# W y of the batch statistics from halves of W and y in three fp32r products, beside one fp32 product, in an attention block on one core

## The reference

```python
x = x + _L0_conv_ref(_gn(x), ...)
# within _L0_conv_ref, per image (n = 4096 positions, c = 256, ci = 128 channels):
g_x  = g_w x + g_b                      # 128 x 4096
attn = softmax(x^T x, axis=-1)          # 4096 x 4096
y    = attn g_x                         # 128 x 4096, transposed back
wy   = W_w y + W_b                      # 256 x 4096
mean, var = wy.mean((0, 2, 3)), wy.var((0, 2, 3))    # over all four images
return (wy - mean) * rsqrt(var + 1e-5) * gamma + beta + x
```

## Time and profile before

| | us |
|---|---|
| median of three runs | 2064.85 (2064.07 to 2065.0) |
| the profiled execution's own time | 2062.11 |
| its span | 2060.4 |
| TensorE busy | 2016.9 (98%) |
| VectorE, ScalarE, GpSimd busy | 1542.7, 1112.0, 788.6 |
| W y for the statistics (L1467), busy as recorded | 50.0 + 14.3, in 98 + 28 recorded instructions |

### The profile page before, as it was taken

One profiled execution on the slowest core, in us unless ns is written; L12 is line 12 of the kernel. 1 busy time (PEld: TensorE's weight loads), 2 busy tenths in 40 slices (PEclk: granted clock), 3 DMA queues, 4 the chain that ended last, 5 costly groups with the idle time before them and its releaser, 6 DMA issues.

```text
span 2060.4 us, 28131 instructions
## 1 busy us (share of the span) xinstructions
PE 2016.9 (98%) x9348; PEld 1453.2 (71%) x9348; DVE 1542.7 (75%) x3116; ACT 1112.0 (54%) x2311; POOL 788.6 (38%) x608
## 2 busy tenths in 40 slices
PE   5999999999999999999999999999999999999999
PEld 4787777666688777766678777766668877776444
DVE  6777777877777777786777777787777777777777
ACT  4345555566444545547554555556644455655657
POOL 3012233469601123358821123246970202345750
PEclk9999999999999999999999999999999999999999
DMA  3222233555511333464622223455561132346998
GB/s 143 106 86 96 102 113 128 179 179 194 169 67 69 126 103 105 160 205 152 219 83 90 83 102 122 128 184 164 188 191 67 67 123 91 103 128 188 344 346 326
DMA packets 107503, 299.90 MB, mean 146 GB/s; under 512 B 11488, under 2 KB 11872, under 8 KB 93536
## 3 DMA queue, kind: packets, MB, share of 16 engines
q1 hardware_dynamic: 107360, 298.11, 42.6%
HBM read 157.55 MB, written 140.51 MB: 145 GB/s over the span
## 4 chain that ended last, share of the span: by engine, by line
PE 89%; ACT 3%; DVE 3%; POOL 2%; issue 2%; DMA 1%; SPq 0%; DVEq 0%; ACTq 0%
PE bank L1397 18%; PE bank L1320 12%; PE bank L1322 12%; PE bank L1321 12%; PE bank L1373 9%; PE bank L1401 5%; PE bank L1403 5%; PE bank L1402 5%; PE bank L1556 3%; PE bank L1467 3%; PE bank L1327 1%; PE bank L1355 1%; PE bank L1356 1%; DVE plo L1127 1%; ACT phi L933 1%
## 5 line engine op out<-in xcount | busy, mean ns | idle before, releaser
L933 ACT CAST phi<-bank 128x512 fp32r<-128x512 f32 x480 | 281.4, 586 | 678.7 <-PE bank L1373 678.3
L1096 DVE TENSOR_SCALAR_CACHE_REDUCE ring<-bank 128x512 f32<-128x512 f32 x560 | 386.2, 690 | 257.0 <-PE bank L1322 200.0
L1320 PE MATMUL bank<-xh 128*128 128x512 f32 (+3 forms) x1152 | 513.4, 446 | 4.0 <-POOL xl L783 3.6
L1322 PE MATMUL bank<-xh,xl 128*128 128x512 f32 (+3 forms) x1152 | 435.4, 378 | 0.0
L1321 PE MATMUL bank<-xl,xh 128*128 128x512 f32 (+3 forms) x1152 | 432.7, 376 | 0.0
L1127 DVE TENSOR_TENSOR plo<-bank,phi 128x512 fp32r<-128x512 f32 x480 | 329.5, 687 | 136.6 <-ACT phi L933 109.4
L892 ACT ACTIVATE ring<-ring,nmax 128x512 f32<-128x512 f32 x464 | 334.7, 723 | 1.0
L812 POOL TENSOR_TENSOR fy_c<-fy_c,maxrow 128x512 f32<-128x512 f32 x192 | 247.6, 1291 | 197.2 <-DMA fy_c<-spill 197.2
L812 POOL TENSOR_TENSOR fy_d<-fy_d,maxrow 128x512 f32<-128x512 f32 x181 | 234.4, 1297 | 230.0 <-DMA fy_d<-spill 230.0
L1373 PEld LDWEIGHTS bank<-ident,ring 128*128 128x128 f32 x1856 | 224.1, 140 | 133.1 <-issue 80.0
L1373 PE MATMUL bank<-ident,ring 128*128 128x128 f32 x1856 | 279.4, 273 | 7.9 <-DVE plo L1127 7.2
(11 more groups left out here) (155 smaller groups left out, 2760.6 us busy)
## 6 DMA issues: line engine op xcount, KB each, us to landing
spill<-ring SPq DMA_DIRECT2D x108, 1024.0 KB, 4.4
fy_c<-spill SPq DMA_DIRECT2D x200, 256.0 KB, 4.0
fy_d<-spill SPq DMA_DIRECT2D x188, 256.0 KB, 4.2
ring<-x_dram SPq DMA_DIRECT2D x42, 512.0 KB, 5.5
lbuf<-spill SPq DMA_DIRECT2D x60, 256.0 KB, 3.8
yd<-yn SPq DMA_DIRECT2D x24, 256.0 KB, 3.3
out_dram<-ring SPq DMA_DIRECT2D x10, 512.0 KB, 3.3
fx_a<-x_dram SPq DMA_DIRECT2D x8, 512.0 KB, 6.9
```

Source lines behind the costliest of these rows:

```text
L933: nc.scalar.copy(phi[:, HI_BUF[n], :], whole(p)).then_inc(hi_made, 1)
L1096: last = nc.vector.tensor_scalar(slot_tile(u, t), src, 1.0, None, ALU.mult, ALU.max, accum_out=rowm[:, t, c:c + 1])
L1320: nc.tensor.matmul(dst, xh[:, k, rows], xh[:, k, cols], start=(k == 0), stop=False)
L1322: last = nc.tensor.matmul(dst, xl[:, k, rows], xh[:, k, cols], start=False, stop=(k == K - 1))
```

## The change

W y for the statistics is made as Wh yh + Wl yh + Wh yl, three fp32r products for each half, instead of one fp32 product. Wh and Wl are made once in the head (ScalarE a copy, GpSimd a subtraction, into wws). For each y, ScalarE casts y to yh (`make_yh`, into yn_r, which is the room of yn; for block 7 into maxrow_r, the room of maxrow) at the head of step 4, and GpSimd takes yl = y - yh (`make_yl`, into lsb_r, the room of lsb) at a place in its queue given by YL_AT. For the y of blocks 0 to 6 VectorE now writes y into row j of colmax in every image (so far in the last one only), and this row is stored. The last y of the last image keeps its fp32 product, as does the final pass, for which W is loaded once more in the last image (WW_BACK). The first half of wy moves from step 5 to step 6, and its bn_stats from step 7 to step 8.

```diff
--- before.py
+++ after.py
@@ -261,7 +261,7 @@
 assert max(NEXT_PRODUCTS) + 1 < TILES + FIRST_EXP
-INVERT_AT, TAKE_AT, SCALE_AT, WY_AT = 0, 1, 2, (5, 9)
+INVERT_AT, TAKE_AT, SCALE_AT, WY_AT = 0, 1, 2, (6, 9)
 LATE = [1] * NB
@@ -324,6 +324,12 @@
              for j in range(1, NB)}
+YL_AT = {j: min(w for w, p in enumerate(LEFT) if p > (j + 1) * TPB + SCALE_AT + LATE[j] + 7) for j in range(NB - 1)}
+WW_BACK = 5 * TPB
+assert WW_BACK > max(G_AT) + 2
+YL_OF = {w: j for j, w in YL_AT.items()}
@@ -457,11 +463,20 @@
             plo = scoped("plo", [P, LOS, W])
+            yn_r = scoped("yn_r", [P, W])
+            maxrow_r = scoped("maxrow_r", [P, W])
+            lsb_r = scoped("lsb_r", [P, W])
+            wgs = scoped("wgs", [P, K, 2 * CI])
         fx_a = sb("fx_a", [P, K, N])
         keep = sb("keep", [P, HIS + LOS, W])
+        yn = sb("yn", [P, W])
+        maxrow = sb("maxrow", [P, W])
+        lsb = sb("lsb", [P, W])
+        wwb = sb("wwb", [P, 2, C])
+        wwt = wwb[:, 0, :]
         ring = sb("ring", [P, SLOTS - 1, T, W])
@@ -490,18 +505,15 @@
         lbuf = sb("lbuf", [P, LBUFS, W])
-        lsb = sb("lsb", [P, W])
-        maxrow = sb("maxrow", [P, W])
-        yn = sb("yn", [P, W])
         ident = sb("ident", [P, P])
         gavg = sb("gavg", [P, P])
-        wgs = sb("wgs", [P, K, 2 * CI], F32R)
         wgh, wgl = wgs[:, :, 0:CI], wgs[:, :, CI:2 * CI]
-        wwt = sb("wwt", [P, C])
+        wws = sb("wws", [P, 2, C], F32R)
+        ww_raw = lsb[:, 0:C]
         bgc = sb("bgc", [P, 2])
         vecs = sb("vecs", [P, 3, K])
-        bst = sb("bst", [P, K, NB, 6])
+        bst = colmax[:, 0, 0:K * NB * 6].rearrange("p (k c s) -> p k c s", k=K, c=NB)
         mv = sb("mv", [P, K, 2])
@@ -580,6 +593,10 @@
         y_stored = sem("y_stored")
+        ww_hi = sem("ww_hi")
+        ww_lo = sem("ww_lo")
+        yh_made = sem("yh_made")
+        yl_made = sem("yl_made")
         wy_made = sem("wy_made")
@@ -646,7 +663,11 @@
-            return colmax[:, j, :] if b == B - 1 and j < NB - 1 else yn[:, :]
+            return colmax[:, j, :] if j < NB - 1 else yn[:, :]
+        def yh_home(j):
+            return (yn_r if j < NB - 1 else maxrow_r)[:, :]
@@ -686,7 +707,7 @@
                 sp.wait_ge(y_made, b * NB + j + 1)
-                sp.dma_start(yd[bass.ds(b, 1), :, j * W:(j + 1) * W].rearrange("b p w -> p (b w)"), yn[:, :]
+                sp.dma_start(yd[bass.ds(b, 1), :, j * W:(j + 1) * W].rearrange("b p w -> p (b w)"), y_home(b, j)
                              ).then_inc(y_stored, 16)
@@ -718,6 +739,9 @@
                     store_y(b - 1, NB - 1)
+                if not more and s == WW_BACK:
+                    sp.wait_ge(g_made, B * (2 * NB))
+                    sp.dma_start(wwt, ww).then_inc(ww_back, 16)
                 if not more and s in FIN_AT:
@@ -741,7 +765,7 @@
             sp.dma_start(wraw, wg.rearrange("(k p) c -> p k c", p=P)).then_inc(consts_in, 16)
-            sp.dma_start(wwt[:, :], ww).then_inc(consts_in, 16)
+            sp.dma_start(ww_raw, ww).then_inc(consts_in, 16)
             sp.dma_start(bgc[:, :], bg).then_inc(consts_in, 16)
@@ -788,10 +812,22 @@
+            def make_yl(b, j):
+                pool.wait_ge(yh_made, b * NB + j + 1)
+                if b + j > 0:
+                    pool.wait_ge(left_summed, b * (NB - 1) + j)
+                nc.gpsimd.tensor_tensor(lsb_r[:, :], y_home(b, j), yh_home(j).bitcast(F32), ALU.subtract
+                                        ).then_inc(yl_made, 1)
             def image(b, more):
+                if b > 0:
+                    make_yl(b - 1, NB - 1)
                 for c in range(len(NEXT_G), NB):
                 for w in range(NLEFT):
+                    if w in YL_OF:
+                        make_yl(b, YL_OF[w])
                     if more and w == AHEAD[GROUP_AT + 4]:
@@ -831,6 +867,8 @@
                 make_gl(0, c)
+            pool.wait_ge(ww_hi, 1)
+            nc.gpsimd.tensor_tensor(wws[:, 1, :], ww_raw, wws[:, 0, :].bitcast(F32), ALU.subtract).then_inc(ww_lo, 1)
             for b in range(B - 1):
@@ -900,6 +938,8 @@
                     act.wait_ge(left_sub_v, sum(v < LEFT_OF[j][0] for v in VSUBS))
+                if j == 1:
+                    act.wait_ge(wy_made, b * (K * NB))
                 nc.scalar.copy(maxrow[:, :], sps).then_inc(maxrow_made, 1)
@@ -935,23 +975,31 @@
                 act.wait_ge(left_added, b * NLEFT + LEFT_OF[j][-1] + 1)
+                act.wait_ge(wy_made, b * (K * NB) + K * j)
                 nc.scalar.copy(lsb[:, :], lacc).then_inc(left_taken, 1)
                 if j > 0:
-                    if b == B - 1:
-                        act.wait_ge(y_made, b * NB + j)
-                    else:
-                        act.wait_ge(wy_made, b * (K * NB) + K * j)
-                        act.wait_ge(y_stored, b * (16 * NB) + 16 * j)
+                    act.wait_ge(wy_made, b * (K * NB) + K * j)
                 nc.scalar.copy(yn[:, :], sps).then_inc(inverse_taken, 1)
+            def make_yh(b, j):
+                act.wait_ge(y_made, b * NB + j + 1)
+                if j == NB - 1:
+                    act.wait_ge(left_sub, pool_subs(b + 1, 0))
+                nc.scalar.copy(yh_home(j), y_home(b, j)).then_inc(yh_made, 1)
                     take_inverse(b - 1, NB - 1)
+                if j >= 1 and i == SCALE_AT + LATE[j - 1] + 1:
+                    make_yh(b, j - 1)
+                if tail and s == SCALE_AT + 2:
+                    make_yh(b - 1, NB - 1)
                 if tail and s == HEAD - 1:
@@ -992,6 +1040,7 @@
                 make_xh(0, c, first=True)
+            nc.scalar.copy(wws[:, 0, :], ww_raw).then_inc(ww_hi, 1)
             for s in range(FIRST_EXP, 0):
@@ -1034,6 +1083,10 @@
                 dve.wait_ge(x_in[c], n * 16 + 16)
+                if n > 0 and c == 0:
+                    dve.wait_ge(y_stored, (n - 1) * (16 * NB) + 16)
+                    dve.wait_ge(yl_made, (n - 1) * NB + 1)
                 for k in range(K):
@@ -1100,6 +1153,10 @@
                         dve.wait_ge(f_taken, n * NPROD + s)
+                    if n > 0 and j == 0 and t == 1:
+                        dve.wait_ge(y_stored, (n - 1) * (16 * NB) + 16 * c)
+                        dve.wait_ge(yl_made, (n - 1) * NB + c)
                     before = slot_tile(u, 0) if j == 0 and t == 1 else cm
@@ -1462,9 +1519,19 @@
-                pe.wait_ge(y_made, b * NB + j + 1)
+                rows = slice(h * P, (h + 1) * P)
                 shared_free(b, "wy", j, h)
-                nc.tensor.matmul(sps, wwt[:, h * P:(h + 1) * P], y_home(b, j), start=True, stop=True
+                if isinstance(b, LastImage) and j == NB - 1:
+                    pe.wait_ge(y_made, b * NB + j + 1)
+                    nc.tensor.matmul(sps, wwt[:, rows], yn[:, :], start=True, stop=True).then_inc(wy_made, 1)
+                    return
+                if b + j == 0:
+                    pe.wait_ge(ww_lo, 1)
+                pe.wait_ge(yh_made, b * NB + j + 1)
+                nc.tensor.matmul(sps, wws[:, 0, rows], yh_home(j), start=True, stop=False)
+                nc.tensor.matmul(sps, wws[:, 1, rows], yh_home(j), start=False, stop=False)
+                pe.wait_ge(yl_made, b * NB + j + 1)
+                nc.tensor.matmul(sps, wws[:, 0, rows], lsb_r[:, :], start=False, stop=True
                                  ).then_inc(wy_made, 1)
@@ -1528,6 +1595,8 @@
+            pe.wait_ge(ww_back, 16)
             def final_wy(u, parts):
```

3 lines of the change are left out of this document (2 added, 1 removed).

## The result

The changed kernel took 2071.74 us (median of 6 executions, 2070.45 to 2073.92), the kernel before 2064.46 us beside it: ratio 1.0036, 95% interval 1.0025 to 1.0047. It is slower by 7.3 us. The forecast was 2064.6 us and "same"; the time lies above its range.

A forecast was written before the change was run, and what follows sets the result against it. TensorE was taken as the bound, one queue busy 2016.9 of 2060.4 us. Products -9.9, low-half pauses +7.8, bn_stats waits +2.4 and give-back -0.5 summed to -0.2 us: 2064.6 us, range 2058.5 to 2070.

The forecast's parts named there:

- The gain of the products: TensorE's wy products: three fp32r products save 0.17 us a half, 9.9 us over 58 halves.
- The pause at the low half: Block 6, images 0 to 2: TensorE waits 2.6 us for the low half in GpSimd's queue, 7.8 us in all.
- what came back behind it: Later small TensorE waits that go away after the pauses: 0.5 us taken, 1.5 us the bound.
- Nothing else behind it was late: Block 6: GpSimd's later subtractions come 1.3 us later, but TensorE is 2.4 us later, so nothing new is late.
- rival 2: ScalarE's wait for y becomes late and holds phi casts behind it: +8 us, 2072 us; chance 13%.
- The wait for bn_stats in block 5: Turned column maxima wait for VectorE's moved bn_stats: 0.65 us, 0.4 in the last image, 2.4 us in all.
- Rival 1: Gain stays: block 6's low-half pause does not come or is given back; 2057.4 us, 2061 with half back; chance 17%.
- 4: Rival: the products don't gain, three accumulated fp32r products being slower than in attend; about +10, 2075 us; chance 2%.
- the main sum: Products' gain, block 6 pauses, block 5 waits and give-back: -9.9 + 7.8 + 2.4 - 0.5 = -0.2 us.
- the three pauses: TensorE's waits for GpSimd's low half in block 6 of images 0 to 2: 3 x 2.6 = 7.8 us.
- rival 3: Pauses worse than counted: TensorE's clock might fall to 1.2 GHz behind them, 15 us for three, 2080 us; chance 8%.
- The last image: Blocks 6 and 7 have TensorE slack: four halves' gain and a 1.7 us low-half pause there were counted as nothing.

The follow-up runs named there:

- the run before: Changed kernel with wy's first half at step 5 except in blocks 6 and 0, and block 6's low half made by VectorE: ratio 1.0017 (0.9986 to 1.0047).

## Why the prediction was wrong

**Right.** The gain of the products, 0.17 us a half, stands in every block without a stall. The pause at the low half was where it was put, for the reason given, and 2.63 us long (forecast 2.6); what came back behind it was 0.18 us in each of three blocks, at step 21, the 0.5 us taken. Nothing else behind it was late, as forecast: steps 13 to 19 of block 6 take what they took. ScalarE's cast costs nothing (rival 2): blocks 1, 3, 4 and 7 would show it. The wait for bn_stats in block 5 was 0.7 us (0.65). Rival 1 and 4 fell.

The mechanism of the main sum was right in kind: a gain, a pause and a wait, each where it was put. The number failed by a cost that the sum put at nothing, and by sizes and places that it missed.

**Wrong: the clock.** The largest step that failed is that the sum charges the three pauses their length and nothing for the clock. It left that to rival 3, which got 8% because "the trace shows full clock throughout" and was priced at 5 us of work at half speed for each pause. In fact six of the nine pauses of 2.6 us in three profiles are followed by 3.4 us at 1.2 GHz, which costs 1.6 us. Of the changed kernel's own profiles one had one such stretch and a clock of 0.999, the other two and 0.998 (3.41 x 0.5 / 2069 is 0.0008 each). Of its twelve executions eight have 0.998 and four 0.999, which makes some 1.7 stretches and 2.7 us in the mean. The prediction also says that no row of the trace has such a gap. One did: in the head TensorE waits 3.6 us, and the score products behind the wait take 0.43 us each (the rows at 22.80 us above). Whether the clock had been up ahead of this wait no row shows. A slice of the page is some 51 us wide, and its 9 in the clock's row does not show these 3 us. A pause of 2.6 us, more than twice the longest recurring wait, should have carried a part of this cost in the main sum.

**Wrong: the size of the stalls.** A wait costs its length and 0.25 us for the first product behind it. Over three pauses in block 6 and four waits in block 5 that is 1.7 us. In the last image the wait in block 5 was 0.7, not 0.4, and 0.05 more in the others: 0.45 us.

**Missing: block 2 and block 0.** TensorE comes 0.2 us too soon for VectorE's addition in block 2, four times, 0.8 us; the forecast looked for places where the moved wy makes others late, not for those where its absence makes TensorE early. Step 25 of block 0 of image 1 is 0.36 us longer, with a wait of 0.16 us for plo (L1430) in it, and was not forecast. VectorE's plo begins late there with no semaphore to wait for:

```profile
649.45 1.47 DVE L1184 TENSOR_TENSOR plo<-bank,phi 128x512 fp32r<-128x512 f32 x2 [0.36 <-issue]
```

In the two profiles with low halves on VectorE the step is not longer (block 0 of image 1 is 0.32 us shorter than before). The cause stays open.

**Sum.** -0.2 + 1.7 + 0.45 + 0.8 + 0.36 = 3.1 us; the blocks up to block 5 of the last image, without the stretch at 1.2 GHz, add up to 3.2. With 2.7 us for the clock it is 5.8 us, where 7.3 and 6.2 were measured; the rest is not assigned.

**The last image** was charged nothing, with some doubt; its blocks 6 and 7 vary by 2 to 3 us without an edit, so neither that zero nor a cost of 1.7 us is shown. The pause for the low half itself was 1.4 us there (forecast 1.7).

**GpSimd.** The forecast said that GpSimd has no idle time in block 6 and let the low half cost a pause only. The runs show the rest: because GpSimd sets the pace there, its 1.3 us are paid at each of the places tried among the block's tiles, and a place further ahead makes the queue wait for ScalarE in other blocks. What can be saved is the difference between 2.6 us with a fall of the clock and some 1.3 us without.

## What to carry to other kernels

Before work is given to the engine with the most idle time over the span, read its windows where the work will stand: GpSimd was busy 38% in all and 100% in the first 45 us of the one block that mattered (953 to 998 us of the kernel before), and there 1.3 us of it cost 1.5 to 4.3 us. Where a product must wait for a new operand, move the product behind work that is ready rather than the operand ahead in an in-order queue; and count a pause of TensorE at its length, a quarter of a microsecond, and what the clock may take behind it. Be wary of giving VectorE an operation with both inputs in SBUF beside a GpSimd that never pauses: here it gave the shortest executions of the study and, in other executions of the same kernel, waits of 21 us.

## What the runs showed of the hardware

- VectorE's subtraction with two SBUF operands (the low half, in the profile with all of them on VectorE) took 0.68 to 0.69 us in the 20 cases where GpSimd idled meanwhile, 1.4 to 1.8 us in ten of the eleven where GpSimd worked, and 22.1 us in the last, until GpSimd's queue broke off. In the run before it took 1.74 us as it got in between two of GpSimd's instructions. The same place in block 6 gave 1.74 us in images 0 and 2 and 22.1 in image 1.
- TensorE's granted clock fell to 1.2 GHz for 3.41 us behind pauses of 1.8 to 2.6 us in some cases and not in others, and in the last image twice behind waits of 0.7 and 1.3 us in a row. In the 22 us event it fell 2.6 us after TensorE's last product (970.2 in that trace), stayed there through the idle time, and rose 5.4 us after work had begun again. At 1.2 GHz a score product takes 0.43 us instead of 0.23.
- A product of fp32r data 128 x 512 takes 0.23 us in the stream with W as the stationary operand as with others, but 0.50 us behind a wait.
